# Both parts of a relative-position bias in one product, its operand packed by transfers within SBUF, in a fused two-layer attention kernel

## The reference

```python
# layer 0: group norm, full attention with decomposed relative positions
q, k, v = heads(x @ Wq + bq), heads(x @ Wk + bk), heads(x @ Wv + bv)
attn = einsum('bqd,bkd->bqk', q, k) / sqrt(64)
rel_bias_h = einsum('bhwc,hkc->bhwk', rq, Rh)      # 32 rows of keys
rel_bias_w = einsum('bhwc,wkc->bhwk', rq, Rw)      # 32 columns of keys
attn = attn + rel_bias_h[..., :, None] + rel_bias_w[..., None, :]
x = x + softmax(attn) @ v @ Wp + bp
# layer 1: group norm, neighbourhood attention, each token over a 7x7 window of keys
x = x + nat_attention(gn(x), qkv_w) @ out_w.T
```

## Time and profile before

| | |
|---|---|
| Time of three runs | 3249.35, 3250.79, 3253.89 us (median 3250.79) |
| The profiled execution | 3253.59 us |
| Its span, first to last instruction | 3251.8 us |
| Mean granted clock of TensorE | 0.991 |
| TensorE busy | 3164.5 us (97%) |
| VectorE busy | 1731.7 us (53%) |
| ScalarE busy | 1228.9 us (38%) |
| GpSimd busy | 1085.2 us (33%) |

### The profile page before, as it was taken

The page is one execution under the profiler, slowest core; times in us unless marked ns, Lnnn a source line. Parts: engine busy times, 40 slices in busy tenths (PEclk is TensorE's granted clock), DMA queues, the critical chain, the costliest instruction groups (busy, mean ns, idle before and its releaser), DMA issues.

```text
span 3251.8 us, 48955 instructions
## 1 busy us (share of the span) xinstructions
PE 3164.5 (97%) x20428; PEld 2368.3 (73%) x20428; DVE 1731.7 (53%) x1889; ACT 1228.9 (38%) x1397; POOL 1085.2 (33%) x618
## 2 busy tenths in 40 slices
PE   8999999999999999999999999999999999999999
PEld 6876658886787665888678756588877876568876
DVE  4447745346434774543644477444473457744435
ACT  2345542224234554213423455321342346532132
POOL 0037770025003776002400477600340047750043
PEclk9999999999999999999999999999999999999999
DMA  3211013113421101311432100121153111022103
GB/s 124 91 36 24 20 45 117 40 53 121 140 99 27 24 20 48 114 40 59 139 134 80 33 21 17 58 104 44 61 165 116 65 34 27 14 88 81 40 24 123
DMA packets 170520, 220.39 MB, mean 68 GB/s; under 512 B 113856, under 2 KB 126400, under 8 KB 170304
## 3 DMA queue, kind: packets, MB, share of 16 engines
q1 hardware_dynamic: 168768, 215.68, 21.2%
q10 hardware_dynamic: 1536, 1.57, 0.2%
HBM read 141.70 MB, written 50.33 MB: 59 GB/s over the span
## 4 chain that ended last, share of the span: by engine, by line
PE 83%; DVE 5%; issue 4%; ACT 3%; SPq 2%; DMA 2%; POOL 1%; ACTq 0%; DVEq 0%; POOLq 0%
PE score L1156 15%; PE score L1157 14%; PE score L1158 14%; PE lot L1313 10%; PE score L1278 9%; PE lot L1228 5%; PE lot L1231 4%; PE score L1285 3%; PE score L1291 3%; SPq L428 2%; DVE recip L931 2%; PE lot L1330 1%; PE lot L1199 1%; PE lot L1261 1%; PE lot L1156 1%
## 5 line engine op out<-in xcount | busy, mean ns | idle before, releaser
L568 POOL TENSOR_TENSOR acc<-acc,prob 128x1024 f32<-128x1024 f32 x288 | 714.9, 2482 | 240.0 <-ACT prob L748 211.3
L748 ACT ACTIVATE prob<-score 128x1024 f32<-128x1024 f32 (+3 forms) x576 | 512.5, 908 | 374.7 <-PE score L1291 296.2
L889 DVE TENSOR_REDUCE max_part<-lot 128x1 f32<-128x512 f32 x640 | 411.1, 684 | 173.4 <-PE lot L1231 173.4
L1313 PE MATMUL lot<-prob,v 128*64 128x512 f32 (+4 forms) x2496 | 470.9, 514 | 7.2 <-ACT o_raw L647 4.4
L1156 PE MATMUL score<-a_hi,w_hi 128*128 128x512 f32 x1152 | 459.1, 399 | 12.9 <-DVE q_lo L1002 5.1
L1157 PE MATMUL score<-a_lo,w_hi 128*128 128x512 f32 x1152 | 450.8, 391 | 0.0
L1158 PE MATMUL score<-a_hi,w_lo 128*128 128x512 f32 x1152 | 450.0, 391 | 0.0
L568 POOL TENSOR_TENSOR acc<-prob 128x1024 f32<-128x1024 f32 x48 | 113.8, 2372 | 860.9 <-ACT prob L748 860.9
L815 DVE TENSOR_TENSOR w_lo<-raw,w_hi 128x1536 fp32r<-128x1536 f32 x95 | 178.8, 1882 | 298.2 <-ACT w_hi L605 297.9
L1156 PE MATMUL score<-w_hi,a_hi 128*128 128x256 f32 x1152 | 336.1, 292 | 0.0
L1313 PEld LDWEIGHTS lot<-prob,v 128*64 128x64 f32 x2496 | 161.5, 136 | 235.9 <-issue 199.1
(11 more groups left out here) (112 smaller groups left out, 5456.5 us busy)
## 6 DMA issues: line engine op xcount, KB each, us to landing
raw<-weights SPq DMA_DIRECT2D x96, 768.0 KB, 4.4
g_mem<-g SPq DMA_DIRECT2D x24, 1024.0 KB, 4.7
xin<-x_t SPq DMA_DIRECT2D x24, 512.0 KB, 6.0
xr<-x_t SPq DMA_DIRECT2D x24, 512.0 KB, 5.0
x_mem<-xr SPq DMA_DIRECT2D x24, 512.0 KB, 6.5
xr<-x_mem SPq DMA_DIRECT2D x24, 512.0 KB, 5.6
y_t<-xr SPq DMA_DIRECT2D x24, 512.0 KB, 6.8
recip<-recip SPq DMA_DIRECT2D x368, 32.0 KB, 1.9
```

Source lines behind the costliest of these rows:

```text
L568: nc.gpsimd.tensor_tensor(acc[:, :, a:b], with_, now, ALU.add).then_inc(added, 1)
L748: nc.scalar.activation(prob[:, ug % P_SLOTS, :, 0:b - a], score[:, u % 2, :, 0:b - a], ACT.Exp, scale=SCALE).then_inc(prob_ok, 1)
L889: nc.vector.reduce_max(max_part[:, t, part, h:h + 1], lot[:, (2 * n + h) % 3, :], AX.X)\
L1313: last = nc.tensor.matmul(lot[rows_of(h), bank, x - half * HALF:y - half * HALF], v[:, t, p * 128 + 64 * h:p * 128 + 64 * h + 64], prob[:, ...
```

## The change

1. The keys of layer 0 are stored in two blocks of 16 columns: a tile of 128 keys is 8 rows by 16 columns. The normalisation writes the input so (`x_norm`); queries are put back into the plain order as they are rounded (ScalarE in one instruction, VectorE's `q_lo` in two). `onehot` is loaded anew in each phase.
2. A tile of keys then meets 8 of 32 rows and 16 of 32 columns. `packed[half]` holds, for each head, 64 partitions: 16 rows of `b_hi`, 16 of `b_lo`, 16 columns of `b_hi`, 16 of `b_lo`, in four combinations for 512 queries. One product with the constant `key_block` replaces the two with `onehot`, from unit 6 (first half) and 10 (second) in pair 0, from unit 3 and 10 in the others (`PACKED_FROM`).
3. `pack(f, p, h)` fills `packed[h]` with 16 transfers on SP's queue, within SBUF, each of 16 partitions by 2×512 numbers (64 KB). It waits for `b_lo` of the pair and for the last unit of the pair before that read that half. SP's order is changed accordingly; weights 10 are asked for in the last pair, behind unit 7, since `packed[0]` takes their slot of memory.
4. `P_SLOTS`, the slots of `prob`, go from 6 to 5, for room.
5. ScalarE: `bias_first` from behind unit 13 to behind unit 10; `out_hi` of the second half from unit 7 to 8; the splits of weights 9 and 10 to units 9 and 13. VectorE: `normalise` of the second half from unit 5 to 7.
6. Layer 1: values in groups of four, behind unit 5 and unit 1 of the next pair; the copy of the output behind unit 2.
7. At the start six matmuls of ones; the first group's means and variances ahead of the later statistics. From layer 1 to the next layer, the product that averages the shifts stands behind the last sums.

```diff
-P_SLOTS = 6
+P_SLOTS = 5
+WARM_UP = 6
+BLOCK = SIDE // 2
+PACKED_FROM = ([6, 10], [3, 10])
@@ SP
+            def pack(f, p, h):
+                s = SET_OF[0][p]
+                sp.wait_ge(b_lo_ok, f // 2 * PAIRS + p + 1)
+                if p:
+                    sp.wait_ge(score_ok, unit_no(f, p - 1, (h + 1) * QT - 1))
+                else:
+                    sp.wait_ge(v_mm, (f + 1) * VN)
+                cols = slice(h * HALF, (h + 1) * HALF)
+                to = packed[h][:, :, :].bitcast(F32).rearrange("p (w r) q -> p w r q", w=2)
+                for n in range(2):
+                    for e, part in enumerate((b_hi[s], b_lo[s])):
+                        for head in range(2):
+                            a, b = 64 * head + BLOCK * n, 64 * head + BLOCK * e
+                            rows = part[a:a + BLOCK, cols].bitcast(F32)
+                            columns = part[a + SIDE:a + SIDE + BLOCK, cols].bitcast(F32)
+                            for dst, src in ((to[b:b + BLOCK, :, n, :], rows),
+                                             (to[b + SIDE:b + SIDE + BLOCK, n, :, :], columns)):
+                                sp.dma_start(dst, src.unsqueeze(1).to_broadcast([BLOCK, 2, HALF]))\
+                                    .then_inc(pack_in[h], 16)
...
                     if p:
                         spread(f, p - 1, 1)
                     if p == LAST:
-                        sp.wait_ge(score_ok, unit_no(f, LAST - 1, 2 * QT - 1))
+                        sp.wait_ge(pack_in[1], packed_no(f, LAST - 1))
                         weights(f, 9)
+                    if p:
+                        pack(f, p, 1)
+                    if p == LAST:
+                        sp.wait_ge(score_ok, unit_no(f, LAST, QT - 1))
+                        weights(f, 10)
                     spread(f, p, 0)
+                    if p < LAST:
+                        pack(f, p + 1, 0)
@@ ScalarE
-                            if u in (5, 13) and p == LAST:
-                                weight_hi(f, QK_CHUNKS + V_CHUNKS + u // 8)
-                            if u == 7 and p:
+                            if u in (9, 13) and p == LAST:
+                                weight_hi(f, QK_CHUNKS + V_CHUNKS + u // 13)
+                            if u == 8 and p:
                                 out_hi(f, p - 1, 1)
...
+                            if u == 10 and ahead:
+                                bias_first(f, p + 2)
...
-                            if u == 13 and ahead:
-                                bias_first(f, p + 2)
@@ VectorE
                     if layer == 0:
-                        nc.vector.scalar_tensor_tensor(dst[:, j % CT, :], src, bqk[:, j:j + 1],
-                                                       hi[:, j % CT, :].bitcast(F32), ALU.add,
-                                                       ALU.subtract).then_inc(qk_lo_ok, 1)
+                        views = [(dst, src, hi)]
+                        if j < CT:
+                            dst, src, hi = by_columns(dst), in_blocks(src), by_columns(hi)
+                            views = [(dst[:, b], src[:, b], hi[:, b]) for b in range(2)]
+                        for dst, src, hi in views:
+                            last = nc.vector.scalar_tensor_tensor(dst, src, bqk[:, j:j + 1], hi, ALU.add,
+                                                                  ALU.subtract)
+                        last.then_inc(qk_lo_ok, 1)
...
-                        if u == 5 and p:
+                        if u == 7 and p:
                             normalise(f, p - 1, 1)
@@ TensorE, in scores()
+                half = u // QT
+                if layer == 0 and u >= PACKED_FROM[p > 0][half]:
+                    if u in PACKED_FROM[p > 0]:
+                        pe.wait_ge(pack_in[half], packed_no(f, p))
+                    combination = (t < QT // 2) * 2 + (t % 4 < 2)
+                    for h in range(2):
+                        last = nc.tensor.matmul(score[:, slot, h, :], key_block[rows_of(h), t % 2, :],
+                                                packed[half][rows_of(h), combination, :],
+                                                start=False, stop=True)
+                    last.then_inc(score_ok, 1)
+                    return
@@ TensorE, layer 1
-                            if u % 2 and u > 1:
-                                values(f, p, u - 3)
-                                values(f, p, u - 2)
+                            if u == GROUPED + 1:
+                                for e in range(GROUPED):
+                                    values(f, p, e)
@@ TensorE, start and turn of layers
+            for n in range(WARM_UP):
+                nc.tensor.matmul(score[:, 0, 0, :], one_column.to_broadcast([128, 128]),
+                                 one_column.to_broadcast([128, HALF]), start=True, stop=True)
             mean_averages(0, 0)
             shift_averages(0, 0)
-            mean_averages(0, 1)
...
-                    if early and c == 0:
-                        shift_averages(f + 1, 0)
                 sums(f, last_pair, PARTS[layer] - 1)
+                if early:
+                    shift_averages(f + 1, 0)
```

More of the change, by code:

```diff
@@ L268, in build @@
     x_next = m.put("x_next", [128, 3, TOKENS], at=slot_at[1])
[L272 removed]
+    bias_at = [m.at, one + 36 * KB, one + 28 * KB, slot_at[1]]
     m.at += 8 * KB
@@ L280, in build @@
         b_lo_raw.append(s != 1 and m.put(f"b_lo_raw{s}", [128, TOKENS], at=at + 4 * KB))
+    packed = [m.put("packed0", [128, 4, HALF], F32R, at=slot_at[0]),
+              m.put("packed1", [128, 4, HALF], F32R, at=one + 36 * KB)]
+    max_wide0 = m.put("max_wide0", [128, 4, 256], F32R, at=slot_at[0] + 8 * KB)
+    onehot_raw = m.put("onehot_raw", [128, TOKENS], at=m.at)
     onehot = m.put("onehot", [128, TOKENS], F32R)
+    key_block = m.put("key_block", [128, 2, 128], F32R)
     ident = m.put("ident", [128, 128], F32R)
@@ L406, in load_bias @@
                     sp.wait_ge(score_ok, unit_no(f, p - 3, 2 * QT - 1))
+                    sp.wait_ge(pack_in[1], packed_no(f, p - 3))
                 else:
@@ L474, in _ @@
                         next_tile(i)
-                weights(f, 10)
+                    weights(f, 10)
+                else:
+                    pack(f, 0, 0)
+                    pack(f, 0, 1)
                 for p in range(PAIRS):
@@ L865, in input_lo @@
                 dve.wait_ge(a_hi_ok, f * CT + i + 1)
-                nc.vector.tensor_tensor(a_lo[:, i, :], xin[:, i, :], a_hi[:, i, :].bitcast(F32),
+                hi, lo = in_halves(f)
+                src = xin[:, i, :] if f % 2 else x_norm[:, i, :]
+                nc.vector.tensor_tensor(lo[:, i, :], src, hi[:, i, :].bitcast(F32),
                                         ALU.subtract).then_inc(a_lo_ok, 1)
@@ L1358, in _ @@
                         project(j, i)
-                        if f % 2 and j == 0 and i == 1:
+                        if len(norm_parts(f)) > 1 and j == 0 and i == 1:
                             mean_averages(f, 1)
-                        if len(norm_parts(f)) > 1 and j == 0 and i == (2 if f else 0):
+                        if len(norm_parts(f)) > 1 and j == 0 and i == 2:
                             shift_averages(f, 1)
@@ L1439, in _ @@
                 last_pair = PAIRS - 1
-                for u in range(UNITS[layer] - (2 if layer else GROUPED), UNITS[layer]):
+                for u in range(UNITS[layer] - GROUPED, UNITS[layer]):
                     values(f, last_pair, u)
@@ L1520 @@
     onehot = np.concatenate([token // SIDE == line[:, None], token % SIDE == line[:, None]]).astype(f32)
+    by_columns = token.reshape(SIDE, 2, BLOCK).transpose(1, 0, 2).reshape(-1)
+    key = np.arange(128)
+    place = np.arange(BLOCK)[::-1, None]
+    columns = np.stack([key % BLOCK == place] * 2, axis=1)
+    rows = np.stack([8 * e + key // BLOCK == place for e in range(2)], axis=1)
+    block = np.concatenate([rows, rows, columns, columns]).astype(f32)
     near = np.clip(np.arange(SIDE), RADIUS, SIDE - 1 - RADIUS)
```

111 lines of the change are left out of this document (72 added, 39 removed).

## The result

The change makes the kernel faster, but by 11 us, not by 46: a median of 3242.94 us (3240.10 to 3244.49, 8 runs) against 3254.15 (3249.35 to 3258.77, 8 runs), a ratio of 0.9966 with the interval 0.9955 to 0.9977. The predicted range was 3166 to 3240. The profiled execution took 3242.22 us, its span is 3240.4 us (3251.8 before), the mean granted clock 0.996 (0.991).

A forecast was written before the change was run, and what follows sets the result against it. The prediction took TensorE's matmuls to bound the kernel (3164.5 of 3251.8 us), with VectorE close behind in places. Its terms, 0 + .8 − 18.6 − 18.6 − 11.9 − 4.5 + 5.5 + .8, gave −46.5: 3204 us, range 3166 to 3240.

The forecast's parts named there:

- The turns: Between layers: moving the shift-averaging product behind the sums removes a 2.27 us stall and 1.7 of clock loss; −11.9 over three.
- That cycle is .68 + .64 + .11 = 1.43.: Layer 0 units with maxima: VectorE's reduce cycle limits a packed unit to 1.43 us against 1.62, saving .18.
- pairs 1 to 3: Layer 0's attention, twelve pairs: segments −.35, +1.4, −.1 and −1.0 were to sum to 0.
- Pair 5, −18.6: Layer 0's last pair: late-weight idle, half rate and eleven products go, two pack waits come; −6.0 in image 0, −4.2 in three.
- Pair 0, −18.6: Layer 0's first pair, four images: shorter bias_first waits and kept clock give −3.0, packed units −.94; −4.6 each.
- Layer 1, +5.5: Layer 1's attention: values grouped by four spare a .27 switch but add .5 of ScalarE waiting; +.23, 24 times.
- the roundings, +.8: q_lo in two halves costs .2 a tile over 24 tiles; +.8 taken, of 4.7 at most.
- The start's −4.5: First projection starts 3.7 us earlier, at 19.5, through the new order; warm-up products give .8 more.
- the first (TensorE takes it all): Whole kernel: no stall for VectorE, matmuls save 57.7 us; −117 in all, 3134 us; chance .07.
- the second (the normalisation costs nothing): Moved second normalisation in layer 0 doesn't stall, its value group coming soon enough: 28 us more off, 3176; chance .15.
- The third (packs late): Pack transfers land late, every pair from 1 waits at unit 3, pair 5 at unit 10 too; slower than before; chance .10.
- The fourth: Clock falls again in pair 0, pair 5 or the transitions since short waits remain: 25 us back, 3229; chance .13.

The follow-up runs named there:

- halved reduce: The changed kernel with VectorE's reduces of the maxima in layer 0 reading 256 of 512 columns: 3203.51 us, ratio 0.9846.
- order alone: The kernel before with bias_first at unit 10, weights 9 and 10 split at 9 and 13, the turn's two moves; no packing, six slots, old start: 3207.55 us.

## Why the prediction was wrong

**The clock and order terms held in the main.** The turns (−11.9, measured −11.1 with the last output), pair 5's two losses and pair 0's half clock went as reckoned. Four terms failed, and together they make nearly all of the 35 us that are missing.

1. **"That cycle is .68 + .64 + .11 = 1.43."** This is the step that failed most, and it is worth some 18 us. The .68 was read where TensorE was not waiting. Where it waits, the first matmul pair starts afresh (.50 for .40, the next one .31 behind, not .23), so from product to reduce it is .76 (302.26, 303.02). The row at 306.44 of the earlier trace rows is such a wait, and the row below, of the kernel before, shows its reduce .77 behind. From the reduce's start back to the next product it is .84 (303.02, 303.86), not .75: the two instructions in the row overlap, the first by itself takes .69 in the trace, not .64, and the product comes .15 behind its end. Together that is 1.60: the very length of an unpacked unit, whereas I had put six products at 1.39 against a cycle of 1.43. So the saving in such a unit is 0, not .18. In pairs 1 to 3: −.02 for −.35 from 1 to 5, +1.64 for +1.4 from 5 to 9, +.03 for −.1 from 9 to 13, −.68 for −1.0 from 13 to 1; a pair +.97 for 0, twelve of them +12. The price of the stall itself was right: without packing beside it, 5 to 9 is 1.87 longer, for the 1.8 reckoned. Pair 4 is +1.1 for +.2, and in pair 0 the packed units give .23 for .94. The halved reduce shows the cause: only with a shorter trip are the products 1.38 apart.

```profile
307.21 1.29 DVE L889 TENSOR_REDUCE max_part<-lot 128x1 f32<-128x512 f32 x2 [0.33 <-PE lot L1231]
```

2. **Pair 5, −18.6, measured −11.6.** The kernel with the order alone, 34.4 us in each image, stands at −17.9; with packing, 6.2 of it came back, where my sum has 3.0 of waits against 2.5 of removed products, so 2.0 in four images. The waits themselves add up to less than reckoned: at unit 3 they are 2.74, 2.06, 3.19 and 1.86 for 1.6, but unit 10 waits only once, .32, for 1.4. In image 0 the sixteen transfers took 12.9 us from the first issue to the last landing, for 11.5 (423.30 to 436.2; the third group of four issues took 3.19 for 2.5, and the last transfer landed 2.7 behind its issue for 2.0). Beside the waits, the clock stood at half for 3.4 us in image 2 (from 2043.0) and in image 3 (from 2848.5). What else makes up the 6.2 isn't split up. That packing is the cause is shown by comparison: in the five kernels without packing in pair 5, the pair takes 34.4 to 35.0 us in every image.

3. **Pair 0, −18.6, measured −12.7.** The clock stayed whole as taken, and the two waits came as reckoned (1.31, and the products 3.04 apart for 3.0). The clock was worth less than the 11.9 that I took: with the .7 an image for the later product as in the sum, some 9. The other 3 are packed units that save nothing, by point 1.

4. **Layer 1, +5.5, measured +8.6, and the roundings, +.8, measured +3.0.** They are right in sign and too small: a pair of layer 1 is +.41 for +.23, and each of layer 0's projections takes 175.3 to 175.5 for 174.4 us.

The start's −4.5 looks right (−4.3), but that is most likely luck. The kernel with the order alone keeps the old start, its first projection at 23.15, and still has its attention begin at 200.72, as the changed kernel at 200.57 and the one before at 204.83; the eleven other kernels with the new start begin theirs between 200.46 and 201.84, none clearly earlier than the old start here. The windows of before and of the order alone differ by the clock's state:

```profile
28.00:32.00 4.00, 4.00 (x13) 3.32 (x13) 1.70 (x3) 1.05 (x2) 0.86 (x1) 1.00 0.00 0
```

```profile
28.00:32.00 4.00, 4.00 (x19) 3.26 (x19) 2.77 (x4) 2.01 (x2) 0.79 (x1) 1.00 0.02 4
```

With 13 matmuls in 4 us for 19, starting .43 apart for .23, the execution before ran there at half rate, and the column of the granted clock says 1.00 for both. The starts, not that column, tell. The earlier start of the changed kernel (19.32) met later waits; what the six warm-up products do by themselves wasn't tried.

Of the rivals, the first (TensorE takes it all) is refuted by the pairs that got longer, and the second (the normalisation costs nothing) by its stall in all 16 pairs. The third (packs late) holds in pair 5 alone: in pairs 1 to 4 unit 3 never waited; these pairs got longer, not shorter. The fourth holds in part: pair 0 kept its clock, but it stood at half for 3.4 us in pair 5 of two images, once in layer 1's attention (2367.2) and once at the third turn (2384.3).

## What to carry to other kernels

Before a matmul is removed, write down the round trip of whatever comes back to TensorE in the same unit, with the start-up of a waiting engine in it (here .76 out, not .68, and .84 back, not .75): if that trip is as long as the unit, the removed product is worth nothing until the trip is made shorter (1.38 a unit with half a reduce). Check moves of order by themselves, since here they made 43 us without the transfers, of which the whole change kept 11. And ask of a late transfer what waits behind it on the same queue: taking away the first wait showed a second.

## What the runs showed of the hardware

VectorE's product of two operands in SBUF takes .68 to .70 us when it meets a gap of GpSimd's additions and up to 2.85 when an addition of 2.4 us has just begun; it ends .55 behind the addition. The prediction took the 1.95 of its row as its length (the mean before is 2.02), where most of it was waiting. The Trainium skill's page "SBUF — State Buffer", section "Who interferes with whom", says that an instruction of VectorE with two SBUF inputs contends with an instruction of GpSimd that reads SBUF, and that "Issue order, not op shape, decides who blocks"; the trace agrees where GpSimd came first, with the 2.85 and the .55 above. VectorE's reduce from PSUM stood at 1.29 for its two halves with additions beside it and without.
